# Three changes to a graph attention kernel: weight maxima spread by TensorE, group 0 transposed graph by graph, the mask multiplied on VectorE

## The chip, the cores and the metric

The kernel runs on one core of a Trainium2 chip. The metric is the device time of one execution in microseconds, and the median over several runs is what counts.

## The reference

For each of 64 graphs with 128 nodes and 512 features, with `h = relu(layernorm(x))`:

```
output = h @ weight ; q = h @ wq ; k = h @ wk
alpha  = max(q @ k^T, 0) * (adj != 0)
alpha  = softmax(alpha, axis=1)      # over n, the first node index
x_out  = x + alpha @ output
```

All inputs are float32 (adj is int32). The three weights are 512x512.

## The kernel before, in words

The 64 graphs are worked in 16 groups of four. `wq` and `wk` enter only through their product, so at the start TensorE transposes both (16 blocks of 128x128 each, float32), multiplies them (`product_m`, 16 float32 products with 512 columns), and everything later uses M = wq wk^T. TensorE works for the groups in float16, and each float32 operand is split into a high and a low part (`_hi`, `_lo`), with three products where float32 would have one. The scores of a group are h M h^T, laid out with m on partitions and n along the free dimension, so that the softmax over n is along the free dimension.

The weights must be scaled by powers of two before they are split. These scales hang on the largest absolute value of each weight. VectorE takes maxima per partition into `w_max` (128x12), GpSimd spreads them over all partitions (`partition_all_reduce`, L295, into `w_maxs`), and VectorE derives `w_scale`, `m_scale` and others in eight small steps counted by `scale_step` (L547 to L566). Then ScalarE makes `w_hi` (L392) and `m_hi` (L395), VectorE `w_lo` (L572) and `m_lo` (L576).

For a group g the work is:

- VectorE: statistics (L430, L434), for a group two ahead in the loop; GpSimd: five small operations to `rstd` and `shift` (`layernorm_scales`); ScalarE: `h` (L329) and `hn_hi` (L337); GpSimd: `hn_lo` (`lo_of_h`, L278).
- SyncE's queue: two DMA transposes per group (L209, `transpose_h`), of `hn_hi` and of `hn_lo`, 128x2048 each, after all four `hn_lo` of the group are made (`h_split`).
- TensorE: `scores(g)` into `s_bank`, `product_v(g, b)` (h weight, for each graph b), `product_t(g+1, c)` (M h^T, for each block c), `product_out(g, b)`, in this order in each turn. Group 0 has its own start: `product_v(0)`, `product_t(0)`, `scores(0)`, `product_t(1)`, `product_out(0)`. `product_v(0)` waits for `w_split`, for both transposes of group 0 and, through `emptied`, for `m_lo`, which has its source in the same banks.
- The mask: VectorE turns `adj` into 0 or -2^127 (`make_mask`, L451), and in `scores` one more product per graph (L634, the mask times a bfloat16 identity) adds it in PSUM.
- The softmax: VectorE takes the row maximum (L457), clamps it (L459) and subtracts it (L461); ScalarE makes one exponential over all four graphs (L352); VectorE sums (L468), scales (L470) and inverts (L475); GpSimd makes `probs`, `p_hi` and `p_lo` (L284 to L289), for which `product_out` waits (`p_split`).
- ScalarE and VectorE empty each of the four banks in two reads (`v_hi` then `v_lo`, `tT_hi` then `tT_lo`), and VectorE adds the residual (L480).

Each engine works through its program in the written order. The queue of SyncE also issues all loads of x and adj and the stores of each graph, in the order of its program: loads of the weights, x and adj of the first groups, then the transposes of group 0, then x of group 3, then the transposes of group 1, and then turn by turn.

Of the kernel before, what the change touches and what calls it, by code (L numbers as in the profile page):

```python
# [5 lines left out]
def graph_attention_kernel(nc, x, adj, weight, wq, wk, out):  # L6
# [32 lines left out]
    MASKED = -2.0 ** 127  # L39
# [38 lines left out]
    with ctx:  # L78
# [12 lines left out]
        mask = sb("mask", [N, 2, GB, N], BF16)  # L91
        h = sb("h", [N, GB, D], F32)
# [19 lines left out]
        ident_bf = sb("ident_bf", [N, N], BF16)  # L112

        w_max = sb("w_max", [N, 3, K], F32)
        w_maxs = sb("w_maxs", [N, 3, K], F32)
# [22 lines left out]
        row_top = sb("row_top", [N, GB], F32)  # L138
        below_max = sb("below_max", [N, GB, N], F32)
# [9 lines left out]
        t_bank = [pb(f"t_bank{k}", [N, K, N], F32) for k in range(2)]  # L149
        s_bank = pb("s_bank", [N, GB, N], F32)  # L150

        start_bank = [t_bank[0], t_bank[1], s_bank, pb("spare_bank", [N, K, N], F32)]
# [10 lines left out]
        ident_bf_made = sem("ident_bf_made")  # L163
        w_maxed = sem("w_maxed")
        w_reduced = sem("w_reduced")
        scale_step = sem("scale_step")
        w_hi_made = sem("w_hi_made")
        w_split = sem("w_split")
        wT_filled = sem("wT_filled")
        wT_copied_act = sem("wT_copied_act")  # L170
        wT_copied_vec = sem("wT_copied_vec")
# [11 lines left out]
        mask_made = sem("mask_made")  # L183
        scores_filled = sem("scores_filled")
        max_found = sem("max_found")
        max_clamped = sem("max_clamped")
        scores_read = sem("scores_read")
        exp_made = sem("exp_made")
        sum_made = sem("sum_made")
# [8 lines left out]
        def _(sp):  # L198
# [33 lines left out]
            for r in range(K):  # L232
                sp.dma_start(wq_sb[:, r], wq[r * N:(r + 1) * N, :]).then_inc(wq_loaded[r], 16)
# [6 lines left out]
            transpose_h(0, 0)  # L240
            load_x(3, 3)
            transpose_h(1, 1)
# [6 lines left out]
        def _(pool):  # L249
            nc.gpsimd.memset(ident[:], 0.0).then_inc(ident_zeroed, 1)  # L250
            nc.gpsimd.memset(ident_bf[:], 0.0).then_inc(ident_zeroed, 1)
# [4 lines left out]
            pool.wait_ge(ident_zeroed, 2)  # L256
            for t, s in ((ident, ident_made), (ident_bf, ident_bf_made)):
                nc.gpsimd.affine_select(out=t[:], in_=t[:], compare_op=ALU.not_equal, fill=1.0, base=0,
                                        pattern=[[-1, N]], channel_multiplier=1).then_inc(s, 1)
# [20 lines left out]
            def normalise(g):  # L280
# [4 lines left out]
                if later(g):  # L285
# [5 lines left out]
            pool.wait_ge(consts_made, 4)  # L291
# [29 lines left out]
        def _(act):  # L321
            for r in range(K):
                act.dma_start(wk_sb[:, r], wk[r * N:(r + 1) * N, :]).then_inc(wk_loaded[r], 16)

# [98 lines left out]
        def _(vec):  # L423
# [106 lines left out]
            for r in range(K):  # L530

                vec.wait_ge(wq_loaded[r], 16)
                if r < 2:
                    weight_max(wq_sb[:, r], w_max[:, 1, r:r + 1])
# [193 lines left out]
```

## Time and profile before

| | |
|---|---|
| median of 3 runs | 472.02 us (471.33 to 472.07) |
| the profiled execution | 471.46 us, of which its span is 469.6 us |
| TensorE busy | 441.9 us, 94% of the span |
| VectorE, ScalarE, GpSimd busy | 237.8, 171.7 and 153.6 us |
| DMA | 57.92 MB, mean 123 GB/s |

The time of the profiled execution is 1.86 us longer than its span; this part lies outside the profile. A busy TensorE is not TensorE at its peak, so the start of each product is a better measure than the busy time.

### The profile page before, as it was taken

Reading aid. Unit: us, or ns where it says so; the run is one execution under the profiler, and the core shown is the slowest. Engines: PE = TensorE matmul, PEld = TensorE weight load, DVE = VectorE, ACT = ScalarE, POOL = GpSimd, SP = SyncE. Lnnn points to the kernel's source line nnn. Section 1 sums busy time; section 2 is a strip of 40 time slices with the busy share of each in tenths; the row PEclk is TensorE's granted clock in tenths of the full one; section 3 lists DMA queues with packets and bytes.
Section 4 is the critical chain, followed back from the end, with each engine's and each line's share of the span. In section 5 each row is a group of like instructions: output and inputs, shape, how many; then the busy total and the mean of one; then the engine's idle time right before and its main releaser. Section 6 shows DMA issues by size and latency. Waiting matters only on the chain.

```text
span 469.6 us, 7193 instructions
## 1 busy us (share of the span) xinstructions
PE 441.9 (94%) x2624; PEld 227.2 (48%) x2624; DVE 237.8 (51%) x457; ACT 171.7 (37%) x285; POOL 153.6 (33%) x205
## 2 busy tenths in 40 slices
PE   5913989999999999999999999999999999999996
PEld 5401454545454544545454545545454545445452
DVE  4680254727364554728364644628273645635254
ACT  3440526261614235262525234261615144261211
POOL 1131145350605243341606143341606143432002
PEclk9975999999999999999999999999999999999999
DMA  8808050837273643718073734618082735224022
GB/s 304 277 0 180 0 114 1 180 120 178 105 180 114 151 141 72 219 22 247 21 187 105 175 115 86 205 37 253 0 215 76 179 112 111 91 52 128 1 89 91
DMA packets 94370, 57.92 MB, mean 123 GB/s; under 512 B 68240, under 2 KB 76432, under 8 KB 94352
## 3 DMA queue, kind: packets, MB, share of 16 engines
q1 hardware_dynamic: 93776, 56.63, 44.1%
q10 hardware_dynamic: 576, 1.05, 0.7%
q8 instruction: 11, 0.18, 0.2%
q14 instruction: 7, 0.06, 0.0%
HBM read 24.12 MB, written 16.78 MB: 87 GB/s over the span
## 4 chain that ended last, share of the span: by engine, by line
PE 91%; issue 3%; DMA 2%; DVE 2%; POOL 1%; SPq 0%; DVEq 0%; ACT 0%; POOLq 0%
PE bank L621 12%; PE bank L623 12%; PE bank L622 12%; PE bank L613 12%; PE bank L612 12%; PE bank L614 12%; PE s_bank L637 3%; PE s_bank L636 3%; PE s_bank L638 3%; PE bank L648 3%; PE bank L647 3%; PE bank L646 3%; DMA hT_lo<-hn_lo 1%; POOL hn_lo L278 1%; PE s_bank L634 1%
## 5 line engine op out<-in xcount | busy, mean ns | idle before, releaser
L621 PE MATMUL bank<-w_hi,hT_hi 128*128 128x512 f16 x256 | 97.9, 383 | 17.2 <-DMA hT_lo<-hn_lo 17.2
L438 DVE SCALAR_TENSOR_TENSOR v_lo<-bank,v_hi 128x512 f16<-128x512 f32 x64 | 44.3, 692 | 111.5 <-ACT v_hi L341 110.0
L622 PE MATMUL bank<-w_lo,hT_hi 128*128 128x512 f16 x256 | 97.8, 382 | 0.0
L623 PE MATMUL bank<-w_hi,hT_lo 128*128 128x512 f16 x256 | 97.8, 382 | 0.0
L612 PE MATMUL bank<-hT_hi,m_hi 128*128 128x512 f16 x256 | 97.1, 379 | 0.0
L613 PE MATMUL bank<-hT_lo,m_hi 128*128 128x512 f16 x256 | 97.1, 379 | 0.0
L614 PE MATMUL bank<-hT_hi,m_lo 128*128 128x512 f16 x256 | 97.1, 379 | 0.0
L278 POOL TENSOR_TENSOR hn_lo<-h,hn_hi 128x512 f16<-128x512 f32 x64 | 73.2, 1157 | 69.8 <-ACT hn_hi L337 62.7
L443 DVE SCALAR_TENSOR_TENSOR tT_lo<-bank,tT_hi 128x512 f16<-128x512 f32 x64 | 44.2, 691 | 92.2 <-ACT tT_hi L345 92.2
L284 POOL TENSOR_TENSOR probs<-exps,row_inv 128x512 f32<-128x512 f32 x16 | 16.6, 1039 | 206.3 <-DVE row_inv L475 206.3
L341 ACT ACTIVATE v_hi<-bank 128x512 f16<-128x512 f32 x64 | 37.9, 592 | 88.7 <-PE bank L623 88.3
L329 ACT ACTIVATE h<-x_sb,shift,rstd 128x512 f32<-128x512 f32 x64 | 50.0, 804 | 38.7 <-POOL shift L273 38.7
L345 ACT ACTIVATE tT_hi<-bank 128x512 f16<-128x512 f32 x64 | 37.7, 589 | 57.2 <-PE bank L614 57.2
L621 PEld LDWEIGHTS bank<-w_hi,hT_hi 128*128 128x128 f16 x256 | 25.2, 98 | 46.9 <-issue 18.9
L352 ACT ACTIVATE exps<-below_max,s_unscale 128x512 f32<-128x512 f32 x16 | 11.5, 722 | 98.3 <-DVE below_max L461 98.3
L636 PE MATMUL s_bank<-tT_hi,hT_hi 128*128 128x128 f16 x256 | 46.2, 219 | 0.0
L638 PE MATMUL s_bank<-tT_hi,hT_lo 128*128 128x128 f16 x256 | 46.2, 219 | 0.0
L637 PE MATMUL s_bank<-tT_lo,hT_hi 128*128 128x128 f16 x256 | 46.2, 219 | 0.0
L480 DVE SCALAR_TENSOR_TENSOR x_sb<-bank,out_unscale,x_sb 128x512 f32<-128x512 f32 x64 | 43.5, 742 | 0.0
L430 DVE BATCH_NORM_STATS2 raw_stats<-x_sb 128x6 f32<-128x512 f32 x64 | 42.1, 675 | 0.0
L623 PEld LDWEIGHTS bank<-w_hi,hT_lo 128*128 128x128 f16 x256 | 25.2, 98 | 30.8 <-issue 1.0
L614 PEld LDWEIGHTS bank<-hT_hi,m_lo 128*128 128x128 f16 x256 | 25.0, 98 | 30.3
(73 smaller groups left out, 484.0 us busy)
## 6 DMA issues: line engine op xcount, KB each, us to landing
x_sb<-in_x SPq DMA_DIRECT2D x16, 1024.0 KB, 5.5
out_h<-x_sb SPq DMA_DIRECT2D x64, 256.0 KB, 2.9
adj_sb<-in_adj SPq DMA_DIRECT2D x16, 256.0 KB, 5.7
wq_sb<-in_L_gnn_wq SPq DMA_DIRECT2D x4, 256.0 KB, 5.0
wk_sb<-in_L_gnn_wk ACTq DMA_DIRECT2D x4, 256.0 KB, 5.4
w_sb<-in_L_gnn_weight SPq DMA_DIRECT2D x1, 1024.0 KB, 11.3
hT_hi<-hn_hi SPq DMA_TRANSPOSE x16, 4.4
hT_lo<-hn_lo SPq DMA_TRANSPOSE x16, 4.9
```

Of the source, the lines that this page charges most:

```text
L278: nc.gpsimd.tensor_tensor(hn_lo[:, s, b], h[:, b], hn_hi[:, s, b], ALU.subtract).then_inc(h_split, 1)
L329: nc.scalar.activation(h[:, b], x_sb[:, s, b], ACT.Relu, bias=shift[:, b:b + 1], scale=rstd[:, b:b + 1]).then_inc(h_made, 1)
L438: nc.vector.scalar_tensor_tensor(v_lo[:, b], bank[b][:], T_SCALE, v_hi[:, b], ALU.mult, ALU.subtract).then_inc(emptied, 1)
L612: nc.tensor.matmul(bank[c][:], mh, hT_hi[:, s, :, k], start=k == 0, stop=False)
L613: nc.tensor.matmul(bank[c][:], mh, hT_lo[:, s, :, k], start=False, stop=False)
L614: last = nc.tensor.matmul(bank[c][:], ml, hT_hi[:, s, :, k], start=False, stop=k == K - 1)
L621: nc.tensor.matmul(bank[b][:], hT_hi[:, s, b, k], w_hi[:, k], start=k == 0, stop=False)
L622: nc.tensor.matmul(bank[b][:], hT_hi[:, s, b, k], w_lo[:, k], start=False, stop=False)
L623: last = nc.tensor.matmul(bank[b][:], hT_lo[:, s, b, k], w_hi[:, k], start=False, stop=k == K - 1)
L636: nc.tensor.matmul(o, hT_hi[:, s, b, k], tT_hi[:, k, b], start=False, stop=False)
L637: nc.tensor.matmul(o, hT_hi[:, s, b, k], tT_lo[:, k, b], start=False, stop=False)
L638: last = nc.tensor.matmul(o, hT_lo[:, s, b, k], tT_hi[:, k, b], start=False, stop=k == K - 1)
```

## The change

Six things are changed.

1. **Loads and transposes of the weights.** The rows of `wk` are loaded and transposed first, then those of `wq`; both are spread over the queues of SyncE and ScalarE (blocks 0 and 2 on the one, 1 and 3 on the other). The transposes use two banks in turn, and ScalarE alone copies them out (8 copies; before, ScalarE and VectorE had four each). `product_m(0)` and `product_m(1)` stand between the transposes of `wq`.
2. **Maxima.** `partition_all_reduce` on GpSimd goes. VectorE reduces `w_max` to three columns (`w_top`), TensorE transposes them to 3x128, VectorE reduces along the row and multiplies a 3x3 identity with the result, and TensorE multiplies that by a 3x128 matrix of ones, which puts the three maxima on every partition. The two small products stand in TensorE's order before and inside `product_m(2)`.
3. **`w_hi`** is made by VectorE, in turn with `w_lo`.
4. **Group 0 is transposed graph by graph**: eight DMA transposes of 128x512, each pair after the `hn_lo` of its graph; `product_v(0, b)` waits for its own graph's. They now stand behind the load of x of group 3 on the queue. In the other groups the transpose of `hn_hi` no longer waits for `hn_lo`.
5. **The mask.** `make_mask` gives 0 or 1, a DMA transpose per group turns it to the layout of the scores (`maskT`), and VectorE multiplies it in where it reads the scores (one `scalar_tensor_tensor` with max and mult). The four mask products per group and the bfloat16 identity go.
6. **The softmax.** The row maximum is taken of the masked scores, its scaled negative is the bias of the exponential, and ScalarE makes four exponentials per group (one for each graph), each with its row sum as accumulator output. The VectorE sum (L468) goes.

```diff
             def transpose_h(g, s):
 
+                sp.wait_ge(h_hi_made, GB * g + GB)
+                sp.dma_start_transpose(hT_hi[:, s].rearrange("p b k n -> p (b k) n"),
+                                       hn_hi[:, s].rearrange("p b d -> p (b d)")).then_inc(hT_landed[s], 16)
                 sp.wait_ge(h_split, GB * g + GB)
-                for hT, hn in ((hT_hi, hn_hi), (hT_lo, hn_lo)):
-                    sp.dma_start_transpose(hT[:, s].rearrange("p b k n -> p (b k) n"),
-                                           hn[:, s].rearrange("p b d -> p (b d)")).then_inc(hT_landed[s], 16)
+                sp.dma_start_transpose(hT_lo[:, s].rearrange("p b k n -> p (b k) n"),
+                                       hn_lo[:, s].rearrange("p b d -> p (b d)")).then_inc(hT_landed[s], 16)
+            def transpose_mask(g, s):
+                sp.wait_ge(mask_made, g + 1)
+                if g >= 2:
+                    sp.wait_ge(scores_read, g - 1)
+                sp.dma_start_transpose(maskT[:, s], mask[:, s].rearrange("p b m -> p (b m)")).then_inc(maskT_landed[s], 16)
+            def transpose_first(b):
+                sp.wait_ge(h_split, b + 1)
+                sp.dma_start_transpose(hT_hi[:, 0, b], hn_hi[:, 0, b]).then_inc(hT0_landed[b], 16)
+                sp.dma_start_transpose(hT_lo[:, 0, b], hn_lo[:, 0, b]).then_inc(hT0_landed[b], 16)
...
                 if more_adj:
-                    sp.wait_ge(mask_made, g + 1)
                     load_adj(g + 2, j % 2)
+                if g + 1 < G:
+                    transpose_mask(g + 1, (j + 1) % 2)
...
-            transpose_h(0, 0)
             load_x(3, 3)
+            for b in range(GB):
+                transpose_first(b)
+            transpose_mask(0, 0)
             transpose_h(1, 1)
...
-            pool.wait_ge(w_maxed, 5)
-            nc.gpsimd.partition_all_reduce(w_maxs[:].rearrange("p w k -> p (w k)"),
-                                           w_max[:].rearrange("p w k -> p (w k)"), N,
-                                           bass.bass_isa.ReduceOp.max).then_inc(w_reduced, 1)
...
             def exponentials(g):
-                act.wait_ge(scores_read, g + 1)
+                act.wait_ge(shift_made, g + 1)
                 if later(g):
                     act.wait_ge(p_split, g)
-                nc.scalar.activation(exps[:], below_max[:], ACT.Exp, scale=s_unscale[:]).then_inc(exp_made, 1)
+                    act.wait_ge(sum_scaled, g)
+                for b in range(GB):
+                    nc.scalar.activation(exps[:, b], alpha[:, b], ACT.Exp, bias=shift_max[:, b:b + 1], scale=s_unscale[:],
+                                         accum_out=row_sum[:, b:b + 1]).then_inc(exp_made, 1)
...
-            for k in range(K):
-                nc.scalar.activation(w_hi[:, k], w_sb[:, k], ACT.Copy, scale=w_scale[:]).then_inc(w_hi_made, 1)
...
                 vec.wait_ge(scores_filled, g + 1)
-                nc.vector.tensor_reduce(row_max[:], s_bank[:], AX.X, ALU.max).then_inc(max_found, 1)
+                vec.wait_ge(maskT_landed[s], 16 * loads)
+                if later(g):
+                    vec.wait_ge(exp_made, GB * g)
+                nc.vector.scalar_tensor_tensor(alpha[:], s_bank[:], 0.0, maskT[:, s], ALU.max,
+                                               ALU.mult).then_inc(scores_read, 1)
+                vec.wait_ge(scores_read, g + 1)
+                nc.vector.tensor_reduce(row_max[:], alpha[:], AX.X, ALU.max).then_inc(max_found, 1)
                 vec.wait_ge(max_found, g + 1)
-                nc.vector.tensor_scalar(row_top[:], row_max[:], 0.0, None, ALU.max).then_inc(max_clamped, 1)
...
+                nc.vector.tensor_scalar(shift_max[:], row_max[:], s_unscale[:], -1.0, ALU.mult,
+                                        ALU.mult).then_inc(shift_made, 1)
...
-            vec.wait_ge(w_reduced, 1)
-            nc.vector.tensor_reduce(w_top[:], w_maxs[:], AX.X, ALU.max).then_inc(scale_step, 1)
+            vec.wait_ge(w_maxed, 2 * K + 1)
+            nc.vector.tensor_reduce(w_top[:], w_max[:], AX.X, ALU.max).then_inc(top_step, 1)
+            vec.wait_ge(top_filled, 1)
+            nc.vector.tensor_reduce(top_col[:], top_bank[0:3, 0:N], AX.X, ALU.max).then_inc(top_step, 1)
+            vec.wait_ge(top_step, 2)
+            nc.vector.tensor_scalar(top_diag[:], ident[0:3, 0:3], top_col[:], None, ALU.mult).then_inc(top_step, 1)
+            vec.wait_ge(top_filled, 2)
+            nc.vector.tensor_copy(w_top[:], top_bank[:, N:N + 3]).then_inc(scale_step, 1)
...
             for k in range(K):
+                nc.vector.tensor_scalar(w_hi[:, k], w_sb[:, k], w_scale[:], None, ALU.mult).then_inc(w_hi_made, 1)
                 vec.wait_ge(w_hi_made, k + 1)
...
-                    nc.tensor.matmul(o, mask[:, s, b], ident_bf[:], start=True, stop=False)
...
             for r in range(K):
-
-                pe.wait_ge(wq_loaded[r], 16)
...
-            pe.wait_ge(wT_copied_act, K)
-            pe.wait_ge(wT_copied_vec, K)
+                transpose_wk(r)
+            transpose_wq(0)
+            transpose_wq(1)
             product_m(0)
+            transpose_wq(2)
+            transpose_wq(3)
             product_m(1)
-            product_m(2)
+            pe.wait_ge(top_step, 1)
+            nc.tensor.transpose(top_bank[0:3, 0:N], w_top[:], ident[:]).then_inc(top_filled, 1)
+            product_m(2, range(2))
+            pe.wait_ge(top_step, 3)
+            pe.wait_ge(consts_made, 5)
+            nc.tensor.matmul(top_bank[:, N:N + 3], ones[:], top_diag[:], start=True, stop=True).then_inc(top_filled, 1)
+            product_m(2, range(2, K))
             product_m(3)
 
             pe.wait_ge(w_split, K)
-            pe.wait_ge(hT_landed[0], 2 * 16)
-            for b in range(GB):
+            for b in range(GB):
+                pe.wait_ge(hT0_landed[b], 2 * 16)
                 product_v(0, 0, b)
```

On VectorE the start is now: eight maxima of 128x512 (`wk`, then `wq`) as the blocks land, the statistics of group 0, the maximum of `w_sb`, and the steps above.

## Rows read from the trace of the kernel before

**Rows 1.** The page: shares of the chain that ended last, by engine.

```profile
PE 91%; issue 3%; DMA 2%; DVE 2%; POOL 1%; SPq 0%; DVEq 0%; ACT 0%; POOLq 0%
```

**Rows 2.** Who TensorE waited for: total us, times, longest.

```profile
PE bank L621 <- DMA hT_lo<-hn_lo: 17.2, 1, 17.2
```

**Rows 3.** The chain that ended last, 17.5 to 35.4 us: start, us, what.

```profile
17.50 5.08 issue
...
23.72 7.00 issue
30.72 4.67 POOL hn_lo L278 x4
```

**Rows 4.** GpSimd's queue under L278: form, ns min/median/max, first and last start.

```profile
L278 POOLq MODIFY_POOL_CONFIG  x2: 102/102/102, 23.6 to 23.6; - x2
```

**Rows 5.** TensorE in time, from the start of the kernel to group 0's scores.

```profile
7.68 1.11 PE L675 MATMUL bank<-ident,wq_sb 128*128 128x128 f32 x4
...
9.17 0.60 PE L675 MATMUL bank<-ident,wq_sb 128*128 128x128 f32 x4
...
11.15 13.97 PE L666 MATMUL bank<-wkT,wqT 128*128 128x512 f32 x32 [0.94 <-DVE wkT L536]
42.35 0.58 PE L621 MATMUL bank<-w_hi,hT_hi 128*128 128x512 f16 x1 [17.22 <-DMA hT_lo<-hn_lo]
...
46.51 0.38 PE L622 MATMUL bank<-w_lo,hT_hi 128*128 128x512 f16 x1
...
66.69 0.22 PE L634 MATMUL s_bank<-ident_bf,mask 128*128 128x128 bf16 x1 [1.46 <-issue]
...
69.59 0.38 PE L612 MATMUL bank<-hT_hi,m_hi 128*128 128x512 f16 x1
```

**Rows 6.** VectorE in time, 12 to 28 us.

```profile
12.05 0.68 DVE L430 BATCH_NORM_STATS2 raw_stats<-x_sb 128x6 f32<-128x512 f32 x1
...
17.53 2.28 DVE L528 TENSOR_REDUCE w_max<-w_sb 128x4 f32<-128x2048 f32 x1
23.68 0.17 DVE L547 TENSOR_REDUCE w_top<-w_maxs 128x3 f32<-128x12 f32 x1 [3.87 <-POOL w_maxs L295]
...
25.71 2.74 DVE L572 SCALAR_TENSOR_TENSOR w_lo<-w_sb,w_scale,w_hi 128x512 f16<-128x512 f32 x4 [0.87 <-ACT w_hi L392]
```

**Rows 7.** ScalarE in time: the first h of group 0, an exponential.

```profile
17.54 1.52 ACT L329 ACTIVATE h<-x_sb,shift,rstd 128x512 f32<-128x512 f32 x2 [7.14 <-POOL shift L273]
...
71.44 0.72 ACT L352 ACTIVATE exps<-below_max,s_unscale 128x512 f32<-128x512 f32 x1 [0.33 <-DVE below_max L461]
```

**Rows 8.** The mask's lines: ns min/median/max, first and last start.

```profile
L634 PE MATMUL s_bank<-ident_bf,mask x64: 216/219/220, 66.7 to 451.7; 128*128 128x128 bf16 x64
L451 DVE TENSOR_SCALAR mask<-adj_sb x16: 416/426/1144, 31.0 to 424.8; 128x512 bf16<-128x512 int32 x16
```

**Rows 9.** DMA issues of the page: KB each, median us to landing.

```profile
w_sb<-in_L_gnn_weight SPq DMA_DIRECT2D x1, 1024.0 KB, 11.3
```

**Rows 10.** The queue of SyncE in time: issues.

```profile
3.06 0.54 SPq L235 DMA_DIRECT2D w_sb<-in_L_gnn_weight  x1
...
63.77 2.79 SPq L209 DMA_TRANSPOSE hT_lo<-hn_lo  x1
...
93.79 0.51 SPq L203 DMA_DIRECT2D adj_sb<-in_adj  x1
```

**Rows 11.** Issues of 9 to 10 us (x of group 2), 63.5 to 65 us (hT_lo).

```profile
x_sb<-in_x SPq DMA_DIRECT2D x1, 1024.0 KB, 12.4
...
hT_lo<-hn_lo SPq DMA_TRANSPOSE x1, 5.0
```

**Rows 12.** A stretch: busy us (x count) by engine, granted clock, DMA share, GB/s.

```profile
29.00:30.00 1.00, 0.00 (x0) 0.00 (x0) 1.00 (x3) 0.73 (x2) 0.00 (x0) 0.68 0.00 0
```

**Rows 13.** The last group: GpSimd's p_lo, and TensorE's first product_out.

```profile
459.74 1.15 POOL L289 TENSOR_TENSOR p_lo<-probs,p_hi 128x512 f16<-128x512 f32 x1
...
462.79 0.38 PE L646 MATMUL bank<-v_hi,p_hi 128*128 128x512 f16 x1
```

More of the change, by code:

```diff
@@ L183, in graph_attention_kernel @@
         mask_made = sem("mask_made")
+        maskT_landed = [sem(f"maskT_landed{s}") for s in range(2)]
         scores_filled = sem("scores_filled")
         max_found = sem("max_found")
-        max_clamped = sem("max_clamped")
+        shift_made = sem("shift_made")
         scores_read = sem("scores_read")
         exp_made = sem("exp_made")
-        sum_made = sem("sum_made")
         sum_scaled = sem("sum_scaled")
@@ L230, in group @@
                     sp.dma_start(out_dram[:, bass.ds(g * GB + b, 1), :], x_sb[:, j, b:b + 1]).then_inc(stored[j], 16)
-            for r in range(K):
+            for r in (0, 2):
+                sp.dma_start(wk_sb[:, r], wk[r * N:(r + 1) * N, :]).then_inc(wk_loaded[r], 16)
+            for r in (0, 2):
                 sp.dma_start(wq_sb[:, r], wq[r * N:(r + 1) * N, :]).then_inc(wq_loaded[r], 16)
@@ L255, in _ @@
             nc.gpsimd.memset(h_scale[:], H_SCALE).then_inc(consts_made, 1)
[L256 to L259, printed above, removed]
+            nc.gpsimd.memset(ones[:], 1.0).then_inc(consts_made, 1)
+            pool.wait_ge(ident_zeroed, 1)
+            nc.gpsimd.affine_select(out=ident[:], in_=ident[:], compare_op=ALU.not_equal, fill=1.0, base=0,
+                                    pattern=[[-1, N]], channel_multiplier=1).then_inc(ident_made, 1)
             def layernorm_scales(g):
@@ L321, in _ @@
         def _(act):
-            for r in range(K):
+            for r in (1, 3):
                 act.dma_start(wk_sb[:, r], wk[r * N:(r + 1) * N, :]).then_inc(wk_loaded[r], 16)
+            for r in (1, 3):
+                act.dma_start(wq_sb[:, r], wq[r * N:(r + 1) * N, :]).then_inc(wq_loaded[r], 16)
             def normalise_h(g, s, b):
@@ L380, in _ @@
             for r in range(K):
-                act.wait_ge(wT_filled, 2 * r + 1)
-                nc.scalar.activation(wqT[:, :, r], bank[r][:].rearrange("p (k n) -> p k n", k=K),
-                                     ACT.Copy).then_inc(wT_copied_act, 1)
+                act.wait_ge(wkT_filled, r + 1)
+                nc.scalar.activation(wkT[:, :, r], wT_bank[r % 2][:], ACT.Copy).then_inc(wkT_copied, 1)
+            for r in range(K):
+                act.wait_ge(wqT_filled, r + 1)
+                nc.scalar.activation(wqT[:, :, r], wT_bank[r % 2][:], ACT.Copy).then_inc(wqT_copied, 1)
             for b in range(GB):
@@ L412, in _ @@
                 hi_of_t(1, c)
[L413 removed]
+                act.wait_ge(hT0_landed[c], 2 * 16)
+                hi_of_h(2, 0, 0, c)
                 if c < 2:
@@ L661, in group, with transpose_wk, transpose_wq @@
                     product_out(g, b)
-            def product_m(c):
+            def transpose_wk(r):
+                pe.wait_ge(wk_loaded[r], 16)
+                if r >= 2:
+                    pe.wait_ge(wkT_copied, r - 1)
                 for k in range(K):
+                    last = nc.tensor.transpose(wT_bank[r % 2][:, k], wk_sb[:, r, k * N:(k + 1) * N], ident[:])
+                last.then_inc(wkT_filled, 1)
+            def transpose_wq(r):
+                pe.wait_ge(wq_loaded[r], 16)
+                if r < 2:
+                    pe.wait_ge(wkT_copied, r + 3)
+                else:
+                    pe.wait_ge(wqT_copied, r - 1)
+                for k in range(K):
+                    last = nc.tensor.transpose(wT_bank[r % 2][:, k], wq_sb[:, r, k * N:(k + 1) * N], ident[:])
+                last.then_inc(wqT_filled, 1)
@@ L666, in product_m @@
+            def product_m(c, ks=range(K)):
+                pe.wait_ge(wkT_copied, K)
+                pe.wait_ge(wqT_copied, c + 1)
+                for k in ks:
                     last = nc.tensor.matmul(bank[c][:], wqT[:, k, c], wkT[:, k], start=k == 0,
                                             stop=k == K - 1)
-                last.then_inc(filled, 1)
+                if k == K - 1:
+                    last.then_inc(filled, 1)
             pe.wait_ge(ident_made, 1)
             for r in range(K):
-                pe.wait_ge(wq_loaded[r], 16)
@@ L674, in _ @@
-                for k in range(K):
-                    last = nc.tensor.transpose(bank[r][:, k * N:(k + 1) * N], wq_sb[:, r, k * N:(k + 1) * N], ident[:])
-                last.then_inc(wT_filled, 1)
-                pe.wait_ge(wk_loaded[r], 16)
-                for k in range(K):
-                    last = nc.tensor.transpose(start_bank[r][:, k], wk_sb[:, r, k * N:(k + 1) * N], ident[:])
-                last.then_inc(wT_filled, 1)
-            pe.wait_ge(wT_copied_act, K)
-            pe.wait_ge(wT_copied_vec, K)
+                transpose_wk(r)
```

70 lines of the change are left out of this document (29 added, 41 removed).

## The prediction

> **What bounds the kernel now.** I read the page's chain of work first: TensorE holds 91% of it [rows 1]. Then who TensorE waited for: after its first loads three waits in the whole execution, 17.2 us before the first `product_v` [rows 2], 1.46 us before the scores of group 0, and 0.94 us before `product_m` [rows 5]. From the scores of group 1 to the end it never waits. So time can come out of two places only: the start, up to the first `product_v` at 42.35 us [rows 5], and the number of TensorE's columns after it.
>
> The chain in time says what the start hangs on [rows 3]. GpSimd stands still for 5.08 us before its `partition_all_reduce` (at 23.2), for 7.00 us after it, and only then makes the four `hn_lo` of group 0 (4.67 us), though ScalarE had finished their sources long before. Two MODIFY_POOL_CONFIG instructions stand at 23.6 us [rows 4]: the 7 us are GpSimd changing its program back. Behind `hn_lo` come the issue and the landing of the two transposes, and TensorE starts at 42.35, released by the second of them [rows 2, 5], with `w_lo` ready since 28.4 [rows 6].
>
> **The change, part by part.** I work out when each of the three inputs of the first `product_v` is there.
>
> *TensorE's own work.* Four transposes show as 1.11 us at 7.68, at half clock, and as 0.60 at 9.17, at full clock, each group overlapping the next by some 0.2 [rows 5]: 0.9 and 0.4 us on the path. With two banks and ScalarE's copy of 0.6 us between fills, I put the six transposes ahead of `product_m(0)` at 9.4 us. Then 13.97 us of products [rows 5], 0.9 us for the last two blocks of `wq`, 0.3 us for the two small products: end at 24.6 (before: 25.12). VectorE's four copies move to ScalarE, which has nothing else then.
>
> *The scales.* x of group 0 is there at about 11.6 us and the statistics take 12.05 to 15.33 [rows 6] now as before, a little earlier as the maxima are done by about 10.4: end at 14.9. The maximum of `w_sb` costs 2.28 us [rows 6], its source having landed at 3.06 + 11.3 = 14.4 [rows 9, 10]: end 17.15. Five steps of 0.17 to 0.2 us each (as L547 [rows 6]) and two small products come behind, but the second product stands behind half of `product_m(2)` (1.75 us) in TensorE's order: the first goes at 17.4 after `product_m(1)`, the second at 19.3. The copy and the seven further steps then end where 23.68 to 24.84 (1.16 us) did before: scales at about 20.8 instead of 24.84. TensorE does not lose by it, because VectorE's two steps (0.4 us) lie under 1.75 us of product.
>
> *`w_hi` and `w_lo`.* They no longer overlap on two engines. A step pair costs 0.42 us (a `tensor_scalar` of 128x512 from SBUF, the median of the mask's [rows 8]) and 0.69 us (2.74 for four [rows 6]), with 0.04 us of semaphore: 4 x 1.15 = 4.6 us, and 0.7 for `m_lo(0)`: 26.1 us if nothing disturbs it. But GpSimd now makes `hn_lo` just then. The trace has one case of that pair: the first mask, at 31.0, beside the `hn_lo` that began at 30.72 [rows 3], took 1.14 us against a median of 0.426 [rows 8], that is, until GpSimd's instruction had ended. Three `hn_lo` of 1.16 us lie in the stretch (the rest of one, 0.55, and two whole): at most 0.55 + 2 x 1.16 = 2.9 us more, 29.0. If only the `tensor_scalar` waits and not `w_lo`, the same interleaving gives 27.6. Bounds 26.1 and 29.0; I take 28.5, nearer to the row.
>
> The Trainium skill, "SBUF — State Buffer", section "Who interferes with whom", says that a VectorE instruction in its two-port mode, and also one with two SBUF inputs against a reading GpSimd, shares one port pair with GpSimd, and that whoever comes second is blocked for the whole of the other's instruction. The mask's row agrees for the first kind; for `w_lo` no row here shows it. By that rule the sum would be 29.0 instead of 28.5.
>
> *hT of group 0.* GpSimd no longer changes its program, so `hn_lo` follows ScalarE. `shift` comes 0.45 us earlier with the statistics, so the chain of h and hn_hi that starts at 17.54 [rows 7] starts at about 17.0, and the first `hn_lo` is made from 19.0 to 20.2. x of group 2 lands at 9.09 + 12.4 = 21.5 [rows 11]. The load of x of group 3 now stands ahead of the transposes, and its 1 MB at the rate of the others (about 2.9 us each) lands near 24.4. A transpose of a quarter of the size costs between a quarter of 5.0 us and the whole [rows 11]; so graph 0 is there between 25.6 and 29.4, and I take 26.5, since the issue of the big one alone takes 2.8 us [rows 10] and should go with the size. Graph 3's follow `hn_lo` 3 (24.9 at the latest) and are needed 7.8 us after the start. This is hidden behind the scales.
>
> So the first `product_v` starts at 28.5, set by VectorE, against 42.35: **13.85 us** less.
>
> *The clock.* After TensorE stopped at 25.12 its granted clock fell between 29 and 30 us: the mean there is 0.68 [rows 12], so of the two levels, 2.4 and 1.2 GHz, it held the upper until about 29.4, 4.2 us after. At 42.35 it began at half clock: from there to 46.51 it got 10 products off, one per 0.43 us, where at full clock one per 0.216 (both in [rows 5]) would have taken 2.16. Now it stands still from 24.6 to 28.5, 3.9 us, less than the 4.2 the trace shows as harmless: **2.0 us** less. The other bound is nothing.
>
> *The mask products.* 64 of them [rows 8]. A product of 128 columns takes a slot of (69.59 - 66.69) / 52 = 0.0558 us [rows 5], as each of them is on the path: **3.6 us** less. Their removal asks for nothing in return on TensorE.
>
> *The mask's transpose.* It is issued in the turn before the scores that need it, just behind the load of adj: at 94.3 in the turn of group 1 [rows 10], for scores that are full at 111.6. Even at the 7 us that the slowest transpose of this trace takes (it is four times as big) it has 10 us in hand. What is queued behind it on SyncE are h's transposes, ten microseconds later. Cost 0; bounds 0 and, where the cover is gone, the whole 7 us per turn.
>
> *The softmax.* VectorE's three steps are the same kinds of work in another order, and the sum (0.65 us) goes. Four exponentials instead of one of 0.72 us [rows 7] cost between 0.72 and 4 x 0.72 = 2.9 us. So p_lo comes between 0.65 earlier and 1.5 later. The tightest place is the last group, where no `product_t` lies between: p_lo is done at 460.89 and wanted at 462.79 [rows 13], 1.9 us in hand. Hidden. The other groups have 10 us more.
>
> *Group 1.* `hT_lo` landed at 63.77 + 5.0 = 68.8 and `product_t(1)` began at 69.59 [rows 10, 11, 5]: 0.8 us in hand. The whole chain (statistics, h, `hn_lo`) moves with `product_v(0)`; statistics of group 1 end at about 35, their `h` waits a microsecond or so more than before, the scores are 0.2 us shorter, but the transpose of `hn_hi` now goes 1.8 us or more ahead of `hn_lo`, so that only one follows it. I see 2 us in hand. Cost 0, other bound 1.5 us.
>
> The 1.46 us before the first scores and the tail stay.
>
> **The sum**, against the profiled execution: 471.46 - 13.85 - 2.0 - 3.6 = 452.0. The median lay 0.56 us above that execution; I say 452.4.
>
> **The rivals.**
>
> - *The clock falls after all.* TensorE stands still 3.9 us by my sum, and 4.4 us by the upper bound of `w_lo`: above 4.2 it starts at half clock again. +2.0: 454.4. For it: the trace shows the fall only once.
> - *No contention.* VectorE and GpSimd slip past each other: `product_v` at 26.1, 2.4 us less: 450.0. Against it: the mask's row.
> - *Small transposes are dear, or the rings are full.* If each of the eight costs what a big one does, its issue at 2 to 2.8 us (about 4.5 a pair), graph 3's land near 40.6 and are wanted at 36.3: 4.1 us more, with graph 0 at 29.4: up to 456.5.
> - *A slow `product_m`.* The first products could run at half clock, since only transposes come ahead of them. 10 slots late by 0.2 us put `product_m(1)`, the small products and the scales 2 us later: 454.4. Against it: four transposes fall from 1.11 to 0.60 us by 9.17 [rows 5], when nothing but transposes had run. The Trainium skill, "TensorE: Matmul & The Clock Gate", part 4 (PE-mode transpose), states that transposes don't count as busy and the full clock isn't engaged for them; the trace disagrees.
> - *The program change stays.* If the 7.00 us on GpSimd had another cause than `partition_all_reduce`, `hn_lo` begins at about 26 and `product_v` near 35.5: 459.
> - *Slower than before.* The mask's transpose, or what it does to the ring, holds up h's transposes or the softmax in each of 15 turns. It decides from 19.4 / 15 = 1.3 us of TensorE waiting per turn, beyond the hand of 9 to 12 us that each has: 473 or more. No row speaks for it.
> - *The start gains nothing* because another thing ends at 42: within 0.2% of before. I see none.
>
> **How the numbers follow.** Chances: the forecast 0.40, its own range 451 to 454 (27.6 to 29.5 for the start, warm); the clock 0.20; no contention 0.15; transposes 0.10; slow `product_m` 0.05; program change 0.05; slower 0.03; no change 0.02. The range of 449.0 to 458.0 takes in the first five cases with their bounds and leaves 0.1 and some of their ends out. A difference of 0.2%, 0.9 us, is about what this measurement can tell from none. Faster: 0.95.
>
> **What would show it.** In the profile after: no MODIFY_POOL_CONFIG and no gap before `hn_lo`; one wait of TensorE of about 4 us ahead of the first `product_v` near 28.5, released by VectorE's `m_lo` or `w_lo`; products there a slot of 0.216 us from the start; `w_hi` steps of which some take over 1 us; a turn of 25.95 us instead of 26.17 for TensorE; no new wait of it later. The prediction is wrong if that wait is released by a DMA transpose, if `product_t(1)` or a `product_out` waits, or if the turns don't shrink by 0.22 us.

## The result, and the profile after

The changed kernel takes 455.16 us (median of 4 runs, 454.48 to 455.64), the kernel before 471.67 beside it. The ratio is 0.9649 with a 95% interval of 0.9632 to 0.9667: 16.5 us less. The profiled execution took 454.48 us with a span of 452.6, against 471.46 and 469.6. The prediction said 452.4, range 449.0 to 458.0. Two of all executions lie far outside the rest (586 us in `busy_gap`, 1667 us of the kernel before beside the first experiments), and no ratio counts them.

Who TensorE waited for in the changed kernel (total us, times, longest):

```profile
PE bank L646 <- DVE m_lo L601: 4.6, 1, 4.6
PE wT_bank L692 <- DMA wk_sb<-in_L_gnn_wk: 4.1, 1, 4.1
PE s_bank L659 <- DVE tT_lo L466: 1.4, 1, 1.4
```

The 17.2 us of [rows 2] are 4.6 us now, and they end with VectorE's `m_lo`, not with a DMA: `product_v(0, 0)` needs only `m_lo(0)`, and that was done at about 29.6. The 1.4 us before the first scores are those of [rows 5]. No turn of the loop has a wait. TensorE in time, from its last `product_m` to the first products of group 1:

```profile
19.75 5.42 PE L711 MATMUL bank<-wkT,wqT 128*128 128x512 f32 x12
29.75 0.59 PE L646 MATMUL bank<-w_hi,hT_hi 128*128 128x512 f16 x1 [4.59 <-DVE m_lo L601]
...
32.54 0.38 PE L647 MATMUL bank<-w_lo,hT_hi 128*128 128x512 f16 x1
...
53.33 0.23 PE L659 MATMUL s_bank<-tT_hi,hT_hi 128*128 128x128 f16 x1 [1.42 <-DVE tT_lo L466]
...
56.02 0.38 PE L637 MATMUL bank<-hT_hi,m_hi 128*128 128x512 f16 x1
```

`product_v` starts at 29.75 instead of 42.35: 12.6 us. From there to the first `product_out` of the last group it is 445.87 - 29.75 = 416.12 us, where it was 462.79 - 42.35 = 420.44 [rows 5, 13]: another 4.3 us. Both together are 16.9 of the 17.0 us between the spans.

The 4.3 us have two parts. From 29.75 to 32.54 seven products go off in 2.79 us, 1.3 more than seven slots of 0.216; before, ten took 2.0 more. That gives 0.7, which is not a gain of the change: the number of slow slots behind this wait is different from trace to trace (7 to 14, see `w_hi` and the clock below). The rest, 3.6, is the mask's products: each turn of the loop takes 25.99 us where it took 26.21, and the scores of group 0 take 56.02 - 53.33 = 2.69 us for 48 products, where 52 took 2.90 [rows 5].

GpSimd and VectorE in the same stretch of the changed kernel:

```profile
19.34 4.72 POOL L300 TENSOR_TENSOR hn_lo<-h,hn_hi 128x512 f16<-128x512 f32 x4 [2.15 <-ACT hn_hi L356]
```

```profile
19.85 0.16 DVE L571 COPY w_top<-top_bank 128x3 f32<-128x3 f32 x1 [1.56 <-PE top_bank L730]
20.05 0.47 DVE L573 TENSOR_SCALAR w_top<-w_top 128x3 f32<-128x3 f32 x1
20.55 0.17 DVE L576 TENSOR_SCALAR pow<-w_top 128x3 int32<-128x3 int32 x1
20.76 1.01 DVE L579 TENSOR_SCALAR ipow<-pow 128x3 int32<-128x3 int32 x1
21.80 0.15 DVE L584 TENSOR_SCALAR w_scale<-ipow 128x1 f32<-128x1 f32 x1
21.88 1.09 DVE L585 SCALAR_TENSOR_TENSOR m_scale<-ipow 128x1 f32<-128x1 f32 x1
22.89 0.14 DVE L588 TENSOR_SCALAR out_unscale<-pow 128x1 f32<-128x1 f32 x1
22.95 1.13 DVE L590 SCALAR_TENSOR_TENSOR s_unscale<-pow 128x1 f32<-128x1 f32 x1
24.11 0.49 DVE L595 TENSOR_SCALAR w_hi<-w_sb,w_scale 128x512 f16<-128x512 f32 x1
24.63 0.75 DVE L597 SCALAR_TENSOR_TENSOR w_lo<-w_sb,w_scale,w_hi 128x512 f16<-128x512 f32 x1
...
28.86 2.72 DVE L601 SCALAR_TENSOR_TENSOR m_lo<-bank,m_scale,m_hi 128x512 f16<-128x512 f32 x4
```

`hn_lo` begins 11.4 us earlier than in [rows 3], and right behind ScalarE. The scale steps, which stood within 1.2 us before, take 4.2 (19.85 to 24.08): three of them, on 128x3 or 128x1 elements, take 1.0 to 1.1 us each. A fourth (L573) takes 0.47. The steps end when GpSimd's last `hn_lo` ends (24.06), and `w_hi` and `w_lo`, which come after, are undisturbed.

Graph 0's transposes of the changed kernel were not the last input. They were issued at 20.52 and 21.86, and landed within 4.3 us of the issue, some 4 us before TensorE started; the six others took 2.5 to 2.6 us each:

```profile
20.52 1.29 SPq L227 DMA_TRANSPOSE hT_hi<-hn_hi  x1
21.86 1.26 SPq L228 DMA_TRANSPOSE hT_lo<-hn_lo  x1
```

### The profile page after: what moved, and what is told of

The parts are those of the page before. It is cut to its first block, busy times and chain, and to the rows that moved or that the text cites. A ratio compares the mean times of both kernels' runs of the same rounds, so it can differ in the third digit from the quotient of the medians.

```text
span 452.6 us, 7240 instructions
## 1 busy us (share of the span) xinstructions
PE 438.3 (97%) x2563; PEld 223.3 (49%) x2563; DVE 230.2 (51%) x448; ACT 190.3 (42%) x397; POOL 152.8 (34%) x203
## 3 DMA queue, kind: packets, MB, share of 16 engines
q10 hardware_dynamic: 576, 1.05, 0.6%
## 4 chain that ended last, share of the span: by engine, by line
PE 95%; DVE 3%; DMA 1%; ACT 0%; issue 0%; DVEq 0%
PE bank L646 12%; PE bank L648 12%; PE bank L647 12%; PE bank L637 12%; PE bank L638 12%; PE bank L639 12%; PE s_bank L659 3%; PE s_bank L660 3%; PE s_bank L661 3%; PE bank L669 3%; PE bank L670 3%; PE bank L671 3%; PE bank L711 2%; PE wT_bank L692 1%; DMA wk_sb<-in_L_gnn_wk 1%; DVE w_lo L597 1%
## 5 line engine op out<-in xcount | busy, mean ns | idle before, releaser
L373 ACT ACTIVATE exps<-alpha,shift_max,s_unscale 128x128 f32<-128x128 f32 x64 | 30.8, 482 | 96.8 <-DVE shift_max L487 96.6
L659 PE MATMUL s_bank<-tT_hi,hT_hi 128*128 128x128 f16 x256 | 43.7, 219 | 1.4 <-DVE tT_lo L466 1.4
L660 PE MATMUL s_bank<-tT_lo,hT_hi 128*128 128x128 f16 x256 | 43.7, 219 | 0.0
L661 PE MATMUL s_bank<-tT_hi,hT_lo 128*128 128x128 f16 x256 | 43.7, 219 | 0.0
L646 PEld LDWEIGHTS bank<-w_hi,hT_hi 128*128 128x128 f16 x256 | 25.2, 98 | 34.0 <-DVE w_lo L597 5.4
L648 PEld LDWEIGHTS bank<-w_hi,hT_lo 128*128 128x128 f16 x256 | 25.2, 98 | 30.5 <-issue 0.5
```

What stands on the lines that cost most here:

```text
L646: nc.tensor.matmul(bank[b][:], hT_hi[:, s, b, k], w_hi[:, k], start=k == 0, stop=False)
L648: last = nc.tensor.matmul(bank[b][:], hT_lo[:, s, b, k], w_hi[:, k], start=False, stop=k == K - 1)
L659: nc.tensor.matmul(o, hT_hi[:, s, b, k], tT_hi[:, k, b], start=k == 0, stop=False)
L660: nc.tensor.matmul(o, hT_hi[:, s, b, k], tT_lo[:, k, b], start=False, stop=False)
L661: last = nc.tensor.matmul(o, hT_lo[:, s, b, k], tT_hi[:, k, b], start=False, stop=k == K - 1)
```

## The experiments

The runs were made in three sets, each beside its own median of the kernel before: the first four experiments (471.37), then `narrow_steps`, `w_hi_scalar`, `busy_gap` and `all_three` (472.09), then `changed_again`, `busy_gap_again` and `steps_and_w_hi` (471.24). Only the last set has the changed kernel in it. Where two experiments differ by a microsecond, I read the ratio and the profile, not the median alone.

### One part of the change at a time

`spread_alone` is the kernel before with the maxima spread by TensorE:

```diff
-            pool.wait_ge(w_maxed, 5)
-            nc.gpsimd.partition_all_reduce(...)
...
+            nc.tensor.transpose(top_bank[0:3, 0:N], w_top[:], ident[:])   # inside product_m(2)
+            nc.tensor.matmul(top_bank[:, N:N + 3], ones[:], top_diag[:], start=True, stop=True)  # behind it
```

> The kernel before with one part of the change: the maxima are spread by TensorE, the rest as before. Theory (the two program changes of GpSimd held hn_lo back): hn_lo of group 0 starts at about 19.5 us instead of 30.7, the two big transposes land near 31.3, the first product_v starts near 31.4 at half clock as before: 11 us less, about 460.5. Rival (the graph by graph transposes are what the start gained by): under 5 us less, 467 or more.

It took 460.48 us, ratio 0.9766 (0.9749 to 0.9782): 10.9 us less. GpSimd:

```profile
19.96 4.72 POOL L284 TENSOR_TENSOR hn_lo<-h,hn_hi 128x512 f16<-128x512 f32 x4 [2.15 <-ACT hn_hi L339]
```

The theory's numbers held: `hn_lo` at 20.0, `product_v` at 31.63. The rival fell: this part alone brings two thirds of the whole.

What the first `product_v` waits for is still the big transpose. The profile names `m_lo`:

```profile
31.63 0.58 PE L629 MATMUL bank<-w_hi,hT_hi 128*128 128x512 f16 x1 [5.34 <-DVE m_lo L584]
```

But it needs only the first of the four `m_lo`, done at 28.82 + 0.74 = 29.56, 2.1 us before:

```profile
28.82 2.72 DVE L584 SCALAR_TENSOR_TENSOR m_lo<-bank,m_scale,m_hi 128x512 f16<-128x512 f32 x4
```

`hT_lo` landed at 26.77 + 4.8 = 31.57, issue and time to landing:

```profile
26.77 2.65 SPq L214 DMA_TRANSPOSE hT_lo<-hn_lo  x1
```

```profile
hT_lo<-hn_lo SPq DMA_TRANSPOSE x1, 4.8
```

The `m_lo` that ended about when TensorE started (31.5) is the fourth, which this product does not wait for.

`first_alone` is the kernel before with group 0 transposed graph by graph, and x of group 3 loaded ahead of it:

```diff
-            transpose_h(0, 0)
             load_x(3, 3)
+            for b in range(GB):
+                transpose_first(b)
```

> The kernel before with one part of the change: group 0 is transposed graph by graph (and x of group 3 loaded ahead of it). Theory: GpSimd still starts hn_lo at 30.7, graph 0 is split at 31.9 and its two transposes land about 4 us later, product_v starts near 36.3 instead of 42.35: 6 us less, about 465.5. With the other part alone at 11 and the mask at 3.6 the three would sum to over 20, more than the 17 of the whole, because the scales take over as the last input. Rival: 10 us or more less, about 461.

It took 466.1 us, ratio 0.9891 (0.9873 to 0.9908): 5.3 us less. TensorE's wait:

```profile
PE bank L630 <- DMA hT_lo<-hn_lo: 12.0, 2, 11.8
```

and on GpSimd

```profile
31.98 4.66 POOL L286 TENSOR_TENSOR hn_lo<-h,hn_hi 128x512 f16<-128x512 f32 x4 [7.10 <-issue]
```

GpSimd's 7.1 us stay, and `hn_lo` comes even later. `product_v` starts at 37.05. The second of the two waits (0.24 us) is for graph 3's last transpose: a pair costs 2.6 us of issue, which is just the pace at which TensorE needs them.

`mask_alone` is the kernel before with parts 5 and 6 (mask and softmax), the start as before:

```diff
-                    nc.tensor.matmul(o, mask[:, s, b], ident_bf[:], start=True, stop=False)
+                nc.vector.scalar_tensor_tensor(alpha[:], s_bank[:], 0.0, maskT[:, s], ALU.max, ALU.mult)
+                    nc.scalar.activation(exps[:, b], alpha[:, b], ACT.Exp, bias=..., accum_out=row_sum[:, b:b + 1])
```

> The kernel before with one part of the change: the mask's transpose, its product on VectorE, the four exponentials with accumulators; the start as before. Theory: only the 64 products of 128 columns go, 0.0558 us each: 3.6 us less, about 468.0, and TensorE waits nowhere new. Rival (the new transpose and the longer ScalarE work cost something in each turn): less than 2.5 us less.

It took 468.21 us, ratio 0.9934 (0.9914 to 0.9954): 3.2 us less, between 2.2 and 4.1. The interval alone does not shut out the rival (less than 2.5), but the profile shows no cost: its span is 465.7, which is 3.9 less than before, and TensorE has no wait that the kernel before hadn't, except 0.6 us for a load at the very start.

The three alone sum to 19.4 us, the whole gives 16.5. `spread_alone` and `first_alone` shorten the same chain (GpSimd, then the transposes). With the maxima spread by TensorE, `product_v` starts at 31.63, set by the transposes, 10.7 us earlier than before. In the changed kernel it starts at 29.75, so there the rest of the change brings the start only 1.9 us more, where `first_alone` had 5.3: the transposes get below `m_lo(0)`, and VectorE is then what the start hangs on. `m_lo(0)` itself was done at 29.6 in both kernels, so parts 1 and 3 (the order of the loads, and `w_hi` on VectorE) together brought it nothing: the spread maxima are read at 19.85 instead of 22.70, and the longer scale steps and `w_hi` on VectorE use that up. What part 1 is worth alone was not tested.

### What slows VectorE's small steps

`lo_after_scales` is the changed kernel with GpSimd's `hn_lo` of group 0 held back until the steps are done:

```diff
             layernorm_scales(0)
+            pool.wait_ge(scale_step, SCALE_STEPS)
             for b in range(GB):
                 lo_of_h(0, 0, b)
```

> The changed kernel, but GpSimd starts hn_lo of group 0 only after VectorE's scale steps are done. Theory (the three steps of 1.0 to 1.1 us waited for GpSimd's hn_lo at the port that both use): all steps take 0.15 to 0.2 us and the scales are done near 21.2 instead of 24.1; in exchange w_hi and w_lo now run beside hn_lo and some take over 1 us; product_v starts between 27.5 and 29.8, the time is 0 to 3 us less than the changed kernel's. Rival (the steps are slow by themselves, or because of the product just read from PSUM): three steps of about 1 us stay and the time stays or grows.

It took 455.88 us, ratio 0.967 (0.9652 to 0.9689), no different from the changed kernel; `product_v` at 30.45. VectorE:

```profile
20.80 0.17 DVE L580 TENSOR_SCALAR ipow<-pow 128x3 int32<-128x3 int32 x1
21.00 0.15 DVE L585 TENSOR_SCALAR w_scale<-ipow 128x1 f32<-128x1 f32 x1
21.07 0.15 DVE L586 SCALAR_TENSOR_TENSOR m_scale<-ipow 128x1 f32<-128x1 f32 x1
...
21.20 0.15 DVE L591 SCALAR_TENSOR_TENSOR s_unscale<-pow 128x1 f32<-128x1 f32 x1
21.39 1.48 DVE L596 TENSOR_SCALAR w_hi<-w_sb,w_scale 128x512 f16<-128x512 f32 x1
22.90 1.52 DVE L598 SCALAR_TENSOR_TENSOR w_lo<-w_sb,w_scale,w_hi 128x512 f16<-128x512 f32 x1
24.35 1.37 DVE L596 TENSOR_SCALAR w_hi<-w_sb,w_scale 128x512 f16<-128x512 f32 x1
25.76 1.52 DVE L598 SCALAR_TENSOR_TENSOR w_lo<-w_sb,w_scale,w_hi 128x512 f16<-128x512 f32 x1
27.20 0.47 DVE L596 TENSOR_SCALAR w_hi<-w_sb,w_scale 128x512 f16<-128x512 f32 x1
```

Without `hn_lo` beside them, all steps take 0.17 us or less: the rival (slow by themselves) fell. With four `hn_lo` beside `w_hi` and `w_lo`, the first four of these take 1.37 to 1.52 us instead of 0.48 and 0.75, and the fifth is fast again. The mechanism held and the gain did not come: each of GpSimd's four instructions held up one of VectorE's, whichever were there. GpSimd lost a little as well, its four `hn_lo` taking 5.3 us instead of 4.72.

The Trainium skill, "SBUF — State Buffer", section "Who interferes with whom", says that a VectorE instruction in its two-port mode, or one with two SBUF inputs beside a GpSimd instruction that reads SBUF, needs ports that GpSimd uses too, and that whichever comes first blocks the other for its whole length. The trace agrees for both kinds, and also for instructions of 128x3 and 128x1 elements, which are held up as long as big ones (1.01 and 1.09 us instead of 0.17 and 0.15).

`narrow_steps` is the changed kernel with the steps written so that none meets that condition:

```diff
-            nc.vector.tensor_copy(w_top[:], top_bank[:, N:N + 3])
-            nc.vector.tensor_scalar(w_top2[:], w_top[:], 2.0 ** -60, 2.0 ** 60, ALU.max, ALU.min)
+            nc.vector.tensor_scalar(w_top2[:], top_bank[:, N:N + 3], 2.0 ** -60, 2.0 ** 60, ALU.max, ALU.min)
...
-            nc.vector.tensor_scalar(ipow2[:].bitcast(I32), pow2[:].bitcast(I32), -1.0, INV_BITS, ALU.mult, ALU.add)
+            for q in range(3):    # pow2 likewise
+                nc.vector.tensor_scalar(ipow2[:, q:q + 1].bitcast(I32), pow2[:, q:q + 1].bitcast(I32), -1.0, INV_BITS,
+                                        ALU.mult, ALU.add)
...
-            nc.vector.scalar_tensor_tensor(m_scale[:], ipow2[:, 1:2], m_factor, ipow2[:, 2:3], ALU.mult, ALU.mult)
+            nc.vector.tensor_scalar(m_scale[:], ipow2[:, 1:2], ipow2[:, 2:3], m_factor, ALU.mult, ALU.mult)
```

> The changed kernel, with the scale steps written so that none has two SBUF tensor inputs or more than one column from SBUF: the first reads PSUM, the two integer steps are three one-column operations each, the two products take their second factor as a scalar. Theory (the port shared with GpSimd): each takes 0.2 us or less although hn_lo runs beside them, the scales are done near 21.4 instead of 24.1; w_hi and w_lo meet the last hn_lo and give some of it back, product_v starts between 27.0 and 28.5: 1.2 to 2.8 us less, and up to 1.3 more if TensorE's clock then has not fallen. Rival: steps stay slow beside hn_lo whatever they read: no change.

It took 453.86 us, ratio 0.961 (0.9576 to 0.9643). GpSimd and VectorE:

```profile
19.96 5.24 POOL L300 TENSOR_TENSOR hn_lo<-h,hn_hi 128x512 f16<-128x512 f32 x4 [2.15 <-ACT hn_hi L356]
```

```profile
20.98 0.28 DVE L579 TENSOR_SCALAR ipow<-pow 128x1 int32<-128x1 int32 x3
...
21.36 0.20 DVE L585 TENSOR_SCALAR m_scale<-ipow 128x1 f32<-128x1 f32 x1
...
21.78 0.85 DVE L595 TENSOR_SCALAR w_hi<-w_sb,w_scale 128x512 f16<-128x512 f32 x1
22.66 1.53 DVE L597 SCALAR_TENSOR_TENSOR w_lo<-w_sb,w_scale,w_hi 128x512 f16<-128x512 f32 x1
24.11 1.37 DVE L595 TENSOR_SCALAR w_hi<-w_sb,w_scale 128x512 f16<-128x512 f32 x1
25.52 0.75 DVE L597 SCALAR_TENSOR_TENSOR w_lo<-w_sb,w_scale,w_hi 128x512 f16<-128x512 f32 x1
```

The steps run at 0.2 us beside `hn_lo`, in the same stretch, so it is what they read and write, and not merely what runs at the same time, that makes them slow. But three of the big ones wait instead (2.0 us in all), and `product_v` starts at 29.45, later than I expected and at half clock. From the first read of `top_bank` to `m_lo(0)` it is 8.1 us instead of 9.0. The gain of the steps is mostly given back. The interval of the ratio overlaps that of the changed kernel's first runs (0.9632 to 0.9667) and just misses that of its second (0.9652 to 0.9688), and the two were not run side by side: a small gain is likely, and not shown.

### `w_hi` and the clock

`w_hi_scalar` is the changed kernel with `w_hi` made by ScalarE, as before:

```diff
-                nc.vector.tensor_scalar(w_hi[:, k], w_sb[:, k], w_scale[:], None, ALU.mult).then_inc(w_hi_made, 1)
...
             act.wait_ge(scale_step, SCALE_STEPS)
+            for k in range(K):
+                nc.scalar.activation(w_hi[:, k], w_sb[:, k], ACT.Copy, scale=w_scale[:]).then_inc(w_hi_made, 1)
```

> The changed kernel, with w_hi made by ScalarE as before. Theory: from the scales (24.1) to m_lo(0) it takes 4.3 us as in the kernel before instead of 5.5, product_v starts near 28.4, and as TensorE then stands still 3.3 us instead of 4.6, it starts at full clock: 1.3 + 1.3 = 2.6 us less. Rival (m_hi behind w_hi on ScalarE makes m_lo late): less than 0.5 us.

It took 452.21 us, ratio 0.9597 (0.9561 to 0.9633), 2.9 us under the changed kernel's median, its span 2.3 us under. TensorE:

```profile
28.70 0.38 PE L647 MATMUL bank<-w_hi,hT_hi 128*128 128x512 f16 x1 [3.17 <-DVE m_lo L602]
28.91 0.38 PE L648 MATMUL bank<-w_lo,hT_hi 128*128 128x512 f16 x1
```

`product_v` starts 1.05 us earlier, and its products follow each other by 0.216 us from the first on: full clock. In this execution part 3 of the change costs about a microsecond by itself and a further 1.3 through the clock. The second does not come every time: three of the five executions have a mean granted clock of 1.000 and took 451.7 to 452.2 us, the two others 0.996, as the changed kernel has it, and 453.4 and 454.0.

`busy_gap` is the changed kernel with four products behind `product_m(3)` that nobody reads:

```diff
             product_m(3)
+            for r in range(4):
+                nc.tensor.matmul(wT_bank[0][:].rearrange("p k n -> p (k n)"), wqT[:, 0, 0], wkT[:, 0], start=True, stop=True)
```

> The changed kernel, with four products of 512 float32 columns into a free bank behind product_m(3), whose result nobody reads: TensorE works until 28.6 instead of 25.1, and product_v starts at 29.75 as before. Theory: it starts at full clock, 1.3 us less (six slots of 0.216 us). Rival (the slow slots are not from the gap): no change.

It took 453.35 us, ratio 0.9605 (0.9574 to 0.9637). I ran it once more, beside the changed kernel:

> The kernel of busy_gap once more, for its profile and beside the changed kernel. Theory: product_v(0) starts at 29.7 to 30.0 us as in the changed kernel, its first products at slots of 0.216 us instead of 0.43, 1.3 us less in all. Rival: slow slots in spite of the filled gap, no difference.

> The changed kernel once more, beside the next two on the same chip, so that small differences can be read. It takes about 455 us.

The changed kernel took 455.3 us (ratio 0.967, 0.9652 to 0.9688), this one 453.52 (0.9625, 0.9609 to 0.9641): 1.8 us less, and the intervals do not touch. TensorE in the second run of `busy_gap`:

```profile
25.42 3.60 PE L734 MATMUL wT_bank<-wkT,wqT 128*128 128x512 f32 x8
30.18 0.38 PE L646 MATMUL bank<-w_hi,hT_hi 128*128 128x512 f16 x1 [1.16 <-DVE m_lo L601]
30.39 0.38 PE L647 MATMUL bank<-w_lo,hT_hi 128*128 128x512 f16 x1
```

and in the second run of the changed kernel:

```profile
30.07 0.58 PE L646 MATMUL bank<-w_hi,hT_hi 128*128 128x512 f16 x1 [4.59 <-DVE m_lo L601]
30.45 0.63 PE L647 MATMUL bank<-w_lo,hT_hi 128*128 128x512 f16 x1
```

The start is the same within 0.1 us, the slots are 0.216 against 0.43, of which the changed kernel has eight here, 1.6 us in all. The theory held: with the gap filled, the first products are fast.

How much a fall of the clock costs is not fixed by the kernel. The slow slots behind the wait are 7 and 8 in the two traces of the changed kernel, 10 in that of the kernel before, 13 in `spread_alone` and 14 in `lo_after_scales`, which lost 1.3, 1.6, 2.0, 2.6 and 2.8 us by them. What decides it, these runs do not show.

### Together

`all_three` joins `narrow_steps`, `w_hi_scalar` and two idle products; `steps_and_w_hi` leaves the idle products out.

> The changed kernel with the three together: steps that need no shared port, w_hi on ScalarE, and two idle products behind product_m(3). Theory: scales at 21.4, w_hi on ScalarE at once, m_lo(0) about 4.3 to 5.5 us later (w_lo still meets hn_lo), product_v between 25.9 and 27.2 at full clock, now close behind TensorE's own work (25.2, with the idle products 26.9): 3.5 to 4.5 us less than the changed kernel, about 451. Rival: the transposes of graph 0 (hi issued 20.5, lo 21.9, landing near 25.4) or the idle products become the last input, and less than 3 us is gained.

> all_three without the idle products. TensorE then stands still from about 25.5 to 27.9, 2.4 us, less than the 3.3 that w_hi_scalar stood still and began at full clock. Theory: as all_three, about 4 us less than the changed kernel, 451. Rival: the idle products carried part of the gain: 452 or more.

The two were run in different sets. `all_three` took 451.04 us (ratio 0.9558, 0.9526 to 0.9589), `steps_and_w_hi` 451.43 (0.9586, 0.9561 to 0.9611). Both have a span of 449.5 us and start `product_v` at 27.89 at full clock. In `steps_and_w_hi`:

```profile
PE bank L647 <- DVE m_lo L602: 2.3, 1, 2.3
```

In the trace this wait of 2.3 us did not lower the clock. That does not settle whether the idle products are needed: three of the five executions took 450.5 to 451.4 us at a mean granted clock of 1.000, the two others 452.7 us at 0.996. `all_three` stayed between 450.5 and 451.4 us, its clock at 0.998 to 1.000, in all five. So the rival is not shut out. Only one trace of each was kept, so where the clock was lower in the two long ones is not shown, and five executions each are few. By its median `steps_and_w_hi` is 3.9 us faster than the changed kernel beside it, and about 4.1% faster than the kernel before.

## Why the prediction was right

The time lies in the range, 2.8 us above the forecast of 452.4 and 1.2 us above the end of its own range (451 to 454). It is the width of the range, which took in the rival of the clock, that holds it. By its steps:

- **The 7 us of GpSimd were a change of its program, made for `partition_all_reduce`**: right in what it costs. With that instruction gone no MODIFY_POOL_CONFIG is left, `hn_lo` starts at 19.34 (19.0 predicted), and `spread_alone` shows 10.9 us for this part by itself. That GpSimd spent the 7 us on its program is read off those two rows alone. The time that it stood still ahead of the instruction was in part a real wait: VectorE's last maximum ended at 19.8 [rows 6], which leaves 3.4 us without a reason in the trace.
- **TensorE's own work ends at 24.6**: half a microsecond short, it ended at 25.17.
- **Scales at 20.8**: wrong. The first read of the spread maxima came at 19.85 (19.6 or so predicted), but the steps took 4.2 us instead of 1.2. I took their length from the kernel before, where GpSimd stood still at that time, and looked for contention only at the big instructions. That put the 3.1 us they lose at nothing.
- **`w_hi` and `w_lo` lose 2.4 us to `hn_lo`**: the mechanism right, the place wrong. They lost nothing, because `hn_lo` was over by then, and no `w_hi` took over 1 us, as it should have by my signs. That the total comes out near is luck in part: what I allowed here covers most of what was lost at the steps. 4 pairs took 4.75 us (4.6 predicted). With 3.1 us lost at the steps against 2.4 allowed here, and half a microsecond of small things, `product_v` starts at 29.75 instead of 28.5: the term of 13.85 us measured 12.6. The upper bound of 29.0 for `m_lo(0)` was 0.6 us short.
- **hT of graph 0 is hidden**: right; in TensorE's order it was there 4 us before.
- **The clock, 2.0 us less**: wrong, this is the rival to which I gave 0.20. TensorE stood still 4.6 us and started at half clock, with seven slow slots where it had been ten, so 0.7 us of the 2.0 came, and that by chance, as the slow slots vary. `busy_gap_again` shows that filling the gap brings the rest. And there was no harmless length of 4.2 us, which I had read off one execution: the clock fell 3.8 us after TensorE's last product here, and 3.1 after in `narrow_steps`.
- **The mask's products, 3.6 us less, all of it kept**: right, 3.6 in the profile, and 3.2 (2.2 to 4.1) in `mask_alone`.
- **The softmax hidden**: right. An exponential of 128x128 takes 0.478 us and its accumulator's read 0.187, four of them 2.0 us instead of 0.72, inside my bounds of 0.72 and 2.9. `p_lo` of the last group was done at 444.28 and wanted at 445.87, 1.6 us in hand (1.9 before).
- **The transpose of the mask hidden**: right; it landed 2.7 to 6.5 us after its issue, and no wait for it shows.
- **Group 1 in time**: right; its `hT_lo` landed at 48.71 + 4.3 = 53.0, and `product_t(1)` began at 56.02, 3 us in hand (2 predicted).
- **`product_m` at full clock from its first product**: right; its first eight records take 3.67 us from 9.55 on and the next eight 3.60. The half clock of the transposes at the very start is read off their durations alone (1.11 us against 0.60 [rows 5]): the granted clock of the profile stands at 1.00 in every stretch from 4 us on.
- **The turns**: they shrink by 0.22 us as forecast, from 26.21 to 25.99; the 26.17 and 25.95 of the prediction were 0.04 off.

In sum: -12.6 (start) - 0.7 (clock) - 3.6 (mask) = -16.9 against -19.45 predicted. The steps that failed are the length of the scale steps and the clock. One slip stands in the sum itself: 452.0 and 0.56 are 452.6, not 452.4.

## What to carry to other kernels

When work is moved so that two engines now run side by side, take the durations of both from a stretch where they do; VectorE's smallest steps can wait as long for GpSimd's instruction as its biggest. A chain that is shortened at two places gives less than the sum, and it pays to name what comes last once both are gone: here it was VectorE, and giving one operation back to the idle ScalarE moved the start further (to 28.70) than the rewriting of the small steps did (29.45). Where a wait has several conditions, look up which of them the waiting instruction really needs; the profile can name another that was signalled at about that time. A wait ahead of TensorE costs twice when the clock falls in it, and whether it falls can differ between executions of one kernel, so look at the granted clock of every execution and not of the profiled one alone.

## What the runs showed of the hardware

- GpSimd's `hn_lo` held up VectorE's instruction whatever the size of the latter: 1.01 us for 128x3, 1.09 and 1.13 for 128x1 with two SBUF inputs, beside `hn_lo` of 1.16. One-column instructions with one tensor input passed at 0.14 to 0.20 us.
- After TensorE stopped, its granted clock fell from the upper to the lower level (2.4 to 1.2 GHz) before the end of waits of 3.7 and 4.6 us, and not, in the traces, in waits of 2.3 and 3.2. The fall came 3.1 us after the last product in `narrow_steps`, 3.8 in the changed kernel and 4.6 in its second trace. Kernels with the short waits had a lower mean clock in two of five executions each (0.996, 1 to 2 us longer), so no length of wait is shown to be safe. Two stretches of one us in the changed kernel, where TensorE had stopped at 25.2:

```profile
28.00:29.00 1.00, 0.00 (x0) 0.00 (x0) 0.96 (x3) 0.00 (x0) 0.00 (x0) 0.98 0.62 127
29.00:30.00 1.00, 0.25 (x1) 0.14 (x2) 1.00 (x2) 0.00 (x0) 0.00 (x0) 0.50 0.35 70
```

- A DMA transpose of 128x512 takes 1.27 us to issue and some 2.5 to land (3.5 and 4.3 for the first two). In the same trace one of 128x2048 takes 1.3 to 3.6 us to issue (median 1.8 for `hT_hi`, 2.5 for `hT_lo`) and 4.3 to 5.4 to land: a quarter of the size costs half or more.
